# An octonion feed-forward kernel: the second x unit of a group placed ahead of its second down unit

## The chip, the cores and the metric

The kernel runs on one core of one Trainium2 chip. The metric is the device time of one execution in microseconds (us), median of several runs.

## What is computed

The input x is 2048 rows of 1024 numbers. With xn the layer norm of x, the output is x + attention(xn) + ffn(xn).

```python
scale = jnp.mean(jnp.abs(W))
Wq = scale * jnp.clip(jnp.round(W / scale), -1.0, 1.0)    # ternary weights
M = jnp.einsum('jik,jod->koid', S_OCT, Wq)                # octonion product as a matrix
y = jnp.einsum('...id,koid->...ko', xp, M)
...
h = jax.nn.silu(gate) * up                                # two such products of xn
out = oct_ternary_linear(hp, w_down)                      # a third one of h
...
x = x + _L0_attn_ref(xn) + _L0_ffn_ref(xn, w_gate, w_up, w_down)
```

The attention part takes each row's circular autocorrelation, weights its six largest lags by a softmax and adds the shifted rows. The lag 0 term outweighs the others so far that the result is xn itself; the kernel computes a bound that shows it for the given rows (units F) and has a slow branch for rows where it doesn't hold. So what is written is x + xn + ffn(xn).

## The kernel before

Rows are worked in G = 8 groups of 256. The work is a hand-written list of **units** (lines 51 to 68), and every engine walks that list with its own part of each unit. For group g and chunk c of the hidden layer (NC = 3 chunks of up to 114):

- G (g, c, Y) and U (g, c, Y): gate and up products of one half Y of the octonion parts. Below, G2.1 is ("G", g, 2, 1), and so on.
- N (g, t): the down product of the 128 rows t; N0 and N1 below. In group g's stretch the N units of group g - 1 are worked.
- X (g, i): transposes of the normalised x of group g into the operand tile xop; X0 and X1 below. In group g's stretch those of group g + 1 are worked.
- F (g): the matmuls of the bound.

A G, U or N unit is a fast algorithm with two halves on TensorE. At its place n in the list TensorE runs the **first half** (16 matmuls at line 311 for G and U, 96 at line 336 for N); ScalarE **copies** the odd quarters out of PSUM (`pk`, line 568); VectorE does the **first adds** (lines 734 to 738) and the **second adds** (lines 750 to 782), four instructions each; then TensorE runs the **second half** (line 318 or 336), at place n + 2, behind the first half of the unit there. After it: for G, ScalarE's silu (lines 593 to 596); for U, VectorE's **product** h (line 838) at place n + 2; for N, VectorE's **residual** (lines 849, 850), at place n + 2 too, and SP's store of the finished tile.

An X unit is 8 transposes on TensorE (line 378), a copy and a rounding on ScalarE (562, 563; one more at 579), and a block of VectorE instructions at once (817, 727 to 766, with a fold at 748 for X1), then 871.

Behind a product h, ScalarE rounds it to f16 (line 539, place n + 3), POOL forms sums and differences (lines 990 to 996), ScalarE rounds these (line 526, at the place that the table round_at gives), and POOL computes the two remainders (lines 998, 1001). POOL works the U units strictly in order. Between two of them, at U0.0 of groups 1 to 6, it computes the normalisation factors of the next group (rstd, lines 964 to 977). ScalarE needs these to normalise x (line 464), and VectorE takes two dots of the normalised rows (line 693) ahead of N0's first adds.

The PSUM accumulator has four places, taken in turn: the unit at place n needs what the unit at n - 4 left there to be gone (`bank_free`): for G its silu, for U its product, for X line 871, for N its residual, for F its minimum.

The loop that TensorE walks:

```python
for n in range(N + 2):
    ...                     # bank_free(unit n - 4), then the first half of unit n
    if n >= 2:
        u = units[n - 2]    # then the second half of unit n - 2
```

SP's queue stores tile t of a group once its residual is done, and behind N1's store loads the two x tiles of the group three ahead (load_x, line 259), then the tile for the next residual.

Of the kernel before, what the change touches and what calls it, by code (L numbers as in the profile page):

```python
def octonion_ffn_attention_kernel(nc, x, w_gate, w_up, w_down, dft, lag, out):
# [15 lines left out]
    G = ROWS // T  # L17
# [33 lines left out]
    units = [("T", 0, 0), ("S", 0), ("X", 0, 0), ("X", 0, 1), ("T", 1, 0), ("S", 1)]  # L51
# [4 lines left out]
    for g in range(1, G):  # L56
        for c in range(NC):
            units += [("G", g, c, 0)]
            if c == 1 or c == 2 and g < G - 1:
                units += [("N", g - 1, c - 1)]  # L60
            units += [("U", g, c, 0)]
            if c and g < G - 1:
                units += [("X", g + 1, c - 1)]
            units += [("G", g, c, 1), ("U", g, c, 1)]
            if c == 2 and g < G - 1:
                units += [("F", g + 1)]

    units += [("N", G - 2, 1)] + [("-", i) for i in range(4)] + [("N", G - 1, 0), ("N", G - 1, 1), ("-", 4), ("R",)]
    N = len(units)
    place = {u: n for n, u in enumerate(units)}  # L70
# [40 lines left out]
    round_at, z_at = {}, {}  # L111
    for u in u_no:
        _, g, c, Y = u
        late = 6 if g == 0 or c == 2 else 4 if (c, Y, g) == (1, 0, G - 1) else 5
        if (g, c) == (G - 1, NC - 1):
            late = 4 + 3 * (1 - Y)
        round_at[place[u] + late] = u
    for _, g, t in n_no:
        z_at[place["N", g, t] + (t if g == G - 1 else 1 if t == 0 else 2 if g == G - 2 else 3)] = (g, t)
    bound_at = place["N", G - 1, 1]  # L120

    ctx = ExitStack()
    with ctx:
# [68 lines left out]
        def bank_pair(n, rows=P):  # L192
            return acc[0:rows, n % 4, :, :]
# [434 lines left out]
        def _(dve):  # L628
# [59 lines left out]
            def dot(g, t):  # L688
                k = NT * g + t
                dve.wait_ge(norm_done, NT * g + NT)  # L690
                if k:
                    dve.wait_ge(dot_done, k)
                nc.vector.scalar_tensor_tensor(dj[:, :], xr[:, t, 0:D // 2], 1.0, xr[:, t, D // 2:D], ALU.mult, ALU.mult,
                                               accum_out=dots[:, k:k + 1]).then_inc(dot_done, 1)
# [22 lines left out]
            def first_adds(n, u):  # L717

                kind, q = u[0], quad_no[u]
                (p0, p1, p2, _), (o1, o3), (b, d) = quad_parts(n, u)  # L720
                if kind == "X" and u[2] == 1:
                    b, d = d, b
                dve.wait_ge(copied, q + 1)
                if q >= 2:
                    dve.wait_ge(y_done, 4 * q - 4)
                if kind == "X":
                    nc.vector.scalar_tensor_tensor(b, p2, XS, o3, ALU.mult, ALU.add).then_inc(l1_done, 1)
                    dve.wait_ge(xlo_done, x_no[u] + 1)
                    nc.vector.scalar_tensor_tensor(p1, p0, XS, o1, ALU.mult, ALU.subtract).then_inc(l1_done, 1)
                    nc.vector.scalar_tensor_tensor(d, p2, XS, o3, ALU.mult, ALU.subtract).then_inc(l1_done, 1)  # L730
                    dve.wait_ge(l1_done, 4 * q + 2)
                    nc.vector.scalar_tensor_tensor(p0, p0, XS, o1, ALU.mult, ALU.add).then_inc(l1_done, 1)
                else:
                    nc.vector.tensor_tensor(b, p2, o3, ALU.add).then_inc(l1_done, 1)  # L734
                    nc.vector.tensor_tensor(p1, p0, o1, ALU.subtract).then_inc(l1_done, 1)
                    nc.vector.tensor_tensor(d, p2, o3, ALU.subtract).then_inc(l1_done, 1)
                    dve.wait_ge(l1_done, 4 * q + 2)
                    nc.vector.tensor_tensor(p0, p0, o1, ALU.add).then_inc(l1_done, 1)  # L738
# [71 lines left out]
            for n in range(N + 2):  # L810
                u = units[n] if n < N else ("",)
                kind = u[0]
                if kind == "X":
                    four = bank_pair(n).rearrange("p b (i t) -> p (b i) t", t=T)
                    at = 4 * u[2]
                    dve.wait_ge(xhi_done, x_no[u] + 1)
                    nc.vector.scalar_tensor_tensor(xop[:, u[1] % 2, at:at + 4, 1, :], four, XS, xop[:, u[1] % 2, at:at + 4, 0, :], ALU.mult, ALU.subtract).then_inc(xlo_done, 1)  # L817
                if u == ("T", 0, 0):
                    dve.wait_ge(w_in[0], 64)
                    half = NJ * NC * DB // 2  # L820
                    nc.vector.tensor_reduce(asum[0:CH, 0, 0:1], stage[0][0:CH, 0:half], AX.X, ALU.add, apply_absolute_value=True).then_inc(abs_done[0], 1)
                    dve.wait_ge(ln_done, 1)
                    nc.vector.tensor_scalar(xr[:, 1, :], xr[:, 1, :], nm[:, 1:2], rs[:, 1:2], ALU.add, ALU.mult).then_inc(norm_done, 1)
                if n in norm_at and kind == "N":
                    dot(norm_at[n], 0)
                    dot(norm_at[n], 1)
                if kind and kind in "GUNX":
                    first_adds(n, u)
                if kind == "X":
                    second_adds(n, u)  # L830
                if n >= 2:
                    v = units[n - 2]
                    if v[0] == "U":
                        m = u_no[v]
                        dve.wait_ge(term_mm, prod_no[v] + 1)
                        dve.wait_ge(silu_done, m + 1)
                        if m < LAST:
                            nc.vector.scalar_tensor_tensor(hx[0:CH, m % 4, :, :], hx[0:CH, m % 4, :, :], (hsc, nhsc)[v[3]][0:CH, :],  # L838
                                                           bank_pair(n - 2, CH).rearrange("p b (i t) -> p (b i) t", t=T), ALU.mult, ALU.mult).then_inc(h_done, 1)
                        else:  # L840
                            split_last(v)
                    elif v[0] == "N":
                        _, g, t = v
                        pair = bank_pair(n - 2).rearrange("p b e -> p (b e)")
                        res = zx[:, t, :]
                        most = D - DB
                        dve.wait_ge(term_mm, prod_no[v] + 1)
                        dve.wait_ge(z_done, n_no[v] + 1)
                        nc.vector.scalar_tensor_tensor(res[:, 0:most], pair[:, 0:most], osc[:, :], res[:, 0:most], ALU.mult, ALU.add)
                        nc.vector.scalar_tensor_tensor(res[:, most:D], pair[:, most:D], nosc[:, :], res[:, most:D], ALU.mult, ALU.add).then_inc(out_done, 1)  # L850
                    elif v[0] == "F":
                        dve.wait_ge(lag_mm, f_no[v] + 1)
                        nc.vector.tensor_reduce(dmin[:, NT * v[1]:NT * v[1] + NT], acc[:, (n - 2) % 4, 1, :].rearrange("p (t l) -> p t l", t=NT),
                                                AX.X, ALU.min).then_inc(bound_done, 1)
                if kind and kind in "GUN":
                    second_adds(n, u)
                if kind == "S":
                    thresholds(n, u[1])
                    if u[1] == 0:
                        up_scales()  # L860
                    if u[1] == 2:
                        out_scales()
                if kind == "R":
                    dve.wait_ge(flag_mm, 1)
                    nc.vector.tensor_copy(flag[:, :], acc[:, n % 4, 0, 0:1]).then_inc(flag_done, 1)
                if 1 <= n <= N:
                    v = units[n - 1]
                    if v[0] == "X":
                        at = NJ + 4 * v[2]
                        dve.wait_ge(xhs_done, x_no[v] + 1)  # L870
                        nc.vector.tensor_tensor(xop[:, v[1] % 2, at:at + 4, 1, :], bank_pair(n - 1).rearrange("p b (i t) -> p (b i) t", t=T),  # L871
                                                xop[:, v[1] % 2, at:at + 4, 0, :], ALU.subtract).then_inc(x_ready, 1)
                    if v[0] == "T":
                        weight_slots(n - 1, v)
                if n in dot_at:
                    dot(*dot_at[n])
                if n == bound_at:
                    bound()
# [158 lines left out]
```

## Time and profile before

| | |
|---|---|
| median of 3 runs | 638.65 us (638.45 to 638.71) |
| the profiled execution | 638.42 us |
| span of its instructions | 636.6 us |
| mean granted TensorE clock | 0.962 |
| busy: PE, DVE, POOL, ACT | 559.4 (88%), 540.0 (85%), 457.6 (72%), 357.2 (56%) |
| chain that ended last, by engine | POOL 47%, issue 28%, DVE 9%, PE 9%, ACT 4% |

Times in the rows count from the span's start. PE is TensorE, DVE VectorE, ACT ScalarE, POOL GpSimd, SP the queue that issues the DMAs. A timeline row gives start, duration, engine, line, operation and, in brackets, how long the engine was idle before it and whose result ended that. The start of the next instruction on an engine can lie some 0.1 us before the printed end of the one ahead, since they are pipelined. Groups 1 to 6 are steady: the same rows come back 67.33 us later. Group 3's stretch of the list shows all of it: G2.0 starts at 312.02, F at 337.66, and G2.0 of the next group at 379.35.

### The profile page before, as it was taken

Reading aid. Unit: us, or ns where it says so; the run is one execution under the profiler, and the core shown is the slowest. Engines: PE = TensorE matmul, PEld = TensorE weight load, DVE = VectorE, ACT = ScalarE, POOL = GpSimd, SP = SyncE. Lnnn points to the kernel's source line nnn. Section 1 sums busy time; section 2 is a strip of 40 time slices with the busy share of each in tenths; the row PEclk is TensorE's granted clock in tenths of the full one; section 3 lists DMA queues with packets and bytes.
Section 4 is the critical chain, followed back from the end, with each engine's and each line's share of the span. In section 5 each row is a group of like instructions: output and inputs, shape, how many; then the busy total and the mean of one; then the engine's idle time right before and its main releaser. Section 6 shows DMA issues by size and latency. Waiting matters only on the chain.

```text
span 636.6 us, 15791 instructions
## 1 busy us (share of the span) xinstructions
PE 559.4 (88%) x6416; PEld 506.8 (80%) x6416; DVE 540.0 (85%) x1293; ACT 357.2 (56%) x503; POOL 457.6 (72%) x356
## 2 busy tenths in 40 slices
PE   0495846938999999999999999999999999999996
PEld 0374634727998899989998999899989998899896
DVE  1998779898989988998988898989899889976864
ACT  4757364537545764586547665575467545553441
POOL 2004837465967999599977997699779986987930
PEclk9777988969999999999999999999999999999999
DMA  9420002001023001120203010300130011002021
GB/s 234 112 68 0 1 1 67 1 0 68 2 68 132 3 2 68 52 83 3 67 2 133 3 60 8 134 1 22 49 133 1 3 67 43 27 2 67 2 69 67
DMA packets 10233, 30.63 MB, mean 48 GB/s; under 512 B 912, under 2 KB 4016, under 8 KB 10160
## 3 DMA queue, kind: packets, MB, share of 16 engines
q1 hardware_dynamic: 9200, 28.22, 13.5%
q10 hardware_dynamic: 960, 1.40, 0.9%
q8 instruction: 50, 0.82, 0.6%
q14 instruction: 23, 0.19, 0.1%
HBM read 21.23 MB, written 8.39 MB: 47 GB/s over the span
## 4 chain that ended last, share of the span: by engine, by line
POOL 47%; issue 28%; DVE 9%; PE 9%; ACT 4%; DMA 1%; POOLq 0%; SPq 0%; ACTq 0%; DVEq 0%
POOL hop L1001 13%; POOL hs L995 9%; POOL hs L996 8%; POOL hs L991 8%; POOL hs L990 6%; PE acc L336 5%; PE acc L318 2%; PE acc L311 2%; DMA xr<-in_x 1%; DVE zx L671 1%; POOL r L966 1%; DVE wd L685 1%; DVE hx L838 1%; ACT junk L459 1%; DVE xop L817 1%
## 5 line engine op out<-in xcount | busy, mean ns | idle before, releaser
L336 PE MATMUL acc<-wd,hop 114*128 114x128 f16 (+1 forms) x2944 | 169.6, 219 | 0.3 <-DVE acc L756 0.2
L336 PEld LDWEIGHTS acc<-wd,hop 114*128 114x128 f16 (+1 forms) x2944 | 166.6, 98 | 1.4 <-DVE acc L756 0.8
L990 POOL TENSOR_TENSOR hs<-hx 114x512 f32<-114x512 f32 x47 | 60.1, 1279 | 94.7 <-DVE hx L838 93.9
L1001 POOL TENSOR_TENSOR hop<-hs,hop 114x1024 f16<-114x1024 f32 x46 | 98.5, 2141 | 36.6 <-ACT hop L526 36.6
L311 PE MATMUL acc<-xop,wg 128*128 128x256 f16 x768 | 98.1, 285 | 19.5 <-DVE zx L671 10.3
L318 PE MATMUL acc<-xop,wg 128*128 128x256 f16 x768 | 94.9, 278 | 16.7 <-DVE acc L774 11.5
L568 ACT ACTIVATE pk<-acc 114x512 f32<-114x512 f32 (+1 forms) x112 | 65.7, 588 | 68.5 <-PE acc L336 34.9
L311 PEld LDWEIGHTS acc<-xop,wg 128*128 128x128 f16 x768 | 77.0, 102 | 32.7 <-DVE zx L671 10.8
L318 PEld LDWEIGHTS acc<-xop,wg 128*128 128x128 f16 x768 | 75.6, 100 | 29.7 <-DVE acc L774 12.5
L998 POOL TENSOR_TENSOR hop<-hx,hop 114x1024 f16<-114x1024 f32 x46 | 99.1, 2154 | 0.0
L311 PE MATMUL acc<-xop,wu 128*128 128x256 f16 x768 | 93.6, 276 | 3.7 <-DVE xop L871 2.9
L318 PE MATMUL acc<-xop,wu 128*128 128x256 f16 x768 | 91.8, 273 | 3.9 <-DVE acc L774 2.9
L539 ACT ACTIVATE hop<-hx 114x1024 f16<-114x1024 f32 x46 | 48.6, 1056 | 73.9 <-DVE hx L838 73.9
L734 DVE TENSOR_TENSOR bd<-acc,pk 114x256 f32<-114x256 f32 (+1 forms) x112 | 47.0, 420 | 48.1 <-ACT pk L568 48.1
L311 PEld LDWEIGHTS acc<-xop,wu 128*128 128x128 f16 x768 | 75.8, 99 | 14.1 <-DVE xop L871 3.2
L318 PEld LDWEIGHTS acc<-xop,wu 128*128 128x128 f16 x768 | 73.8, 98 | 14.6 <-DVE acc L774 3.6
L526 ACT ACTIVATE hop<-hs 114x1024 f16<-114x1024 f32 x46 | 48.5, 1055 | 46.9 <-POOL hs L996 46.9
L838 DVE SCALAR_TENSOR_TENSOR hx<-hx,few,acc 114x1024 f32<-114x1024 f32 x47 | 59.8, 1272 | 6.4 <-PE acc L318 3.3
L995 POOL TENSOR_TENSOR hs<-hs 114x512 f32<-114x512 f32 x47 | 62.4, 1328 | 3.7
L996 POOL TENSOR_TENSOR hs<-hs 114x512 f32<-114x512 f32 x47 | 62.4, 1328 | 0.0
L991 POOL TENSOR_TENSOR hs<-hx 114x512 f32<-114x512 f32 x47 | 60.0, 1277 | 0.0
L738 DVE TENSOR_TENSOR acc<-acc,pk 114x256 f32<-114x256 f32 (+1 forms) x112 | 47.3, 422 | 0.0
(133 smaller groups left out, 824.3 us busy)
## 6 DMA issues: line engine op xcount, KB each, us to landing
xr<-in_x SPq DMA_DIRECT2D x16, 512.0 KB, 4.8
zx<-in_x SPq DMA_DIRECT2D x16, 512.0 KB, 3.7
out_y<-zx SPq DMA_DIRECT2D x16, 512.0 KB, 2.9
hop<-in_w_down SPq DMA_DIRECT2D x1, 1364.0 KB, 18.1
hop<-in_w_gate ACTq DMA_DIRECT2D x1, 1152.0 KB
hop<-in_w_up SPq DMA_DIRECT2D x1, 1152.0 KB
hop<-in_w_gate ACTq DMA_DIRECT2D x1, 192.0 KB
hop<-in_w_up SPq DMA_DIRECT2D x1, 192.0 KB
```

The lines of the kernel that those rows point to most:

```text
L311: last = nc.tensor.matmul(acc[:, n % 4, s // 2, T * (s % 2):T * (s % 2 + 1)], wm[:, c, slot, :], xop[:, g % 2, form, level, :], start=s // ...
L318: last = nc.tensor.matmul(acc[:, n % 4, s // 2, T * (s % 2):T * (s % 2 + 1)], wm[:, c, slot, :], xop[:, g % 2, form, level, :], start=Fals ...
L336: last = nc.tensor.matmul(acc[:, n % 4, s // 2, at:at + P], operand(g, c, t, form, level), wd[0:WIDE[c], slot, c, :], start=which == 0 and ...
L539: nc.scalar.activation(half_of(g, c, 4 * Y, 0), by_tile(h), ACT.Copy).then_inc(hhi_done, 1)
L568: nc.scalar.activation(pk[0:rows, q % 2, :, :], pair[0:rows, :, T:2 * T], ACT.Copy).then_inc(copied, 1)
L838: nc.vector.scalar_tensor_tensor(hx[0:CH, m % 4, :, :], hx[0:CH, m % 4, :, :], (hsc, nhsc)[v[3]][0:CH, :], bank_pair(n - 2, CH).rearrange( ...
L990: nc.gpsimd.tensor_tensor(hs[:, 4:8:2, :], h[:, 0:4:2, :], h[:, 1:4:2, :], ALU.add)
L991: nc.gpsimd.tensor_tensor(hs[:, 5:8:2, :], h[:, 0:4:2, :], h[:, 1:4:2, :], ALU.subtract).then_inc(hpair_done, 1)
L995: nc.gpsimd.tensor_tensor(hs[:, 0:2, :], hs[:, 4:6, :], hs[:, 6:8, :], ALU.add).then_inc(hs_done, 1)
L996: nc.gpsimd.tensor_tensor(hs[:, 2:4, :], hs[:, 4:6, :], hs[:, 6:8, :], ALU.subtract).then_inc(hs_done, 1)
L998: nc.gpsimd.tensor_tensor(half_of(g, c, 4 * Y, 1), by_tile(h), half_of(g, c, 4 * Y, 0), ALU.subtract).then_inc(h_free, 1)
L1001: nc.gpsimd.tensor_tensor(half_of(g, c, NJ + 4 * Y, 1), by_tile(hs[:, 0:4, :]), half_of(g, c, NJ + 4 * Y, 0), ALU.subtract).then_inc(h_rea ...
```

## The change

In the stretch of groups 1 to 6 the part of the list for chunk 2 was G2.0, N1, U2.0, X1, G2.1, U2.1, F; it becomes G2.0, X1, N1, U2.0, G2.1, U2.1, F. The table round_at puts the rounding of U1.0's sums six places behind its unit instead of five, and that of U2.0's sums five behind instead of six, which is the same place of the list as before, since U2.0 itself moved by one. z_at puts ScalarE's preparation of N1's residual (line 515) one place behind N1 instead of three, one place earlier in the list than before. On VectorE the second adds of a G unit now stand ahead of the residual of an N unit two places back: G2.1 in groups 1 to 6, G1.1 in group 7.

```diff
--- before.py
+++ after.py
@@ -56,11 +56,13 @@
     for g in range(1, G):
         for c in range(NC):
             units += [("G", g, c, 0)]
+            if c == 2 and g < G - 1:
+                units += [("X", g + 1, 1)]
             if c == 1 or c == 2 and g < G - 1:
                 units += [("N", g - 1, c - 1)]
             units += [("U", g, c, 0)]
-            if c and g < G - 1:
-                units += [("X", g + 1, c - 1)]
+            if c == 1 and g < G - 1:
+                units += [("X", g + 1, 0)]
             units += [("G", g, c, 1), ("U", g, c, 1)]
             if c == 2 and g < G - 1:
                 units += [("F", g + 1)]
@@ -112,11 +114,13 @@
     for u in u_no:
         _, g, c, Y = u
         late = 6 if g == 0 or c == 2 else 4 if (c, Y, g) == (1, 0, G - 1) else 5
+        if 0 < g < G - 1 and Y == 0 and c:
+            late = 7 - c
         if (g, c) == (G - 1, NC - 1):
             late = 4 + 3 * (1 - Y)
         round_at[place[u] + late] = u
     for _, g, t in n_no:
-        z_at[place["N", g, t] + (t if g == G - 1 else 1 if t == 0 else 2 if g == G - 2 else 3)] = (g, t)
+        z_at[place["N", g, t] + (t if g == G - 1 else 1 if t == 0 or g < G - 2 else 2)] = (g, t)
     bound_at = place["N", G - 1, 1]
 
     ctx = ExitStack()
@@ -826,7 +830,9 @@
                     dot(norm_at[n], 1)
                 if kind and kind in "GUNX":
                     first_adds(n, u)
-                if kind == "X":
+
+                ahead = kind == "G" and n >= 2 and units[n - 2][0] == "N"
+                if ahead or kind == "X":
                     second_adds(n, u)
                 if n >= 2:
                     v = units[n - 2]
@@ -852,7 +858,7 @@
                         dve.wait_ge(lag_mm, f_no[v] + 1)
                         nc.vector.tensor_reduce(dmin[:, NT * v[1]:NT * v[1] + NT], acc[:, (n - 2) % 4, 1, :].rearrange("p (t l) -> p t l", t=NT),
                                                 AX.X, ALU.min).then_inc(bound_done, 1)
-                if kind and kind in "GUN":
+                if kind and kind in "GUN" and not ahead:
                     second_adds(n, u)
                 if kind == "S":
                     thresholds(n, u[1])
```

TensorE, groups 1 to 6 (here group 1), from G2.0's first half to the first F matmul. In this view 311 and 318 are first and second halves (`wg` a G unit, `wu` a U unit), 336 a half of an N unit, 378 an X unit. Before:

```order
L311 MATMUL acc<-xop,wg 128x256 x16
L318 MATMUL acc<-xop,wg 128x256 x16
L336 MATMUL acc<-wd,hop 128x128 x96
L318 MATMUL acc<-xop,wu 128x256 x16
L311 MATMUL acc<-xop,wu 128x256 x16
L318 MATMUL acc<-xop,wg 128x256 x16
L378 MATMUL acc<-ident,xr 128x128 x8
L336 MATMUL acc<-wd,hop 128x128 x96
L311 MATMUL acc<-xop,wg 128x256 x16
L318 MATMUL acc<-xop,wu 128x256 x16
L311 MATMUL acc<-xop,wu 128x256 x16
L389 MATMUL acc<-xop,dft_sb 128x256
```

With the change (its line numbers are 4 higher):

```order
L315 MATMUL acc<-xop,wg 128x256 x16
L322 MATMUL acc<-xop,wg 128x256 x16
L382 MATMUL acc<-ident,xr 128x128 x8
L322 MATMUL acc<-xop,wu 128x256 x16
L340 MATMUL acc<-wd,hop 128x128 x96
L322 MATMUL acc<-xop,wg 128x256 x16
L315 MATMUL acc<-xop,wu 128x256 x16
L315 MATMUL acc<-xop,wg 128x256 x16
L340 MATMUL acc<-wd,hop 128x128 x96
L315 MATMUL acc<-xop,wu 128x256 x16
L322 MATMUL acc<-xop,wu 128x256 x16
L393 MATMUL acc<-xop,dft_sb 128x256
```

The transposes stand directly behind G1.1's second half, ahead of both halves of N1. G2.1's first half now precedes N1's second half, and U2.0's second half comes behind U2.1's first half instead of behind G2.1's.

ScalarE at the same place, from the silu of G1.1. 526 rounds the sums of a U unit, 539 its product; `pk` copies are 568 (128 rows: N1) and 562 (X1), 563 and 579 round x parts, 593 and 594 are the silu of G2.0, 515 prepares N1's residual. Before:

```order
L596 ACTIVATE hx<-acc,few 114x1024 [waits h_free,term_mm]
L526 ACTIVATE hop<-hs 114x2x4x128 [waits hs_done]
L568 ACTIVATE pk<-acc 128x512 [waits spec_mm,l1_done]
L539 ACTIVATE hop<-hx 114x2x4x128 [waits term_mm,h_done]
L568 ACTIVATE pk<-acc 114x512 [waits spec_mm,l1_done]
L593 ACTIVATE hx<-acc,few 114x768 [waits h_free,term_mm]
L594 ACTIVATE hx<-acc,few 114x256
L562 ACTIVATE pk<-acc 128x512 [waits x_mm,l1_done]
L563 ACTIVATE xop<-acc 128x4x256
L515 ACTIVATE zx<-zx,nmrs,onep 128x1024 [waits zx_in1]
L526 ACTIVATE hop<-hs 114x2x4x128 [waits hs_done]
L568 ACTIVATE pk<-acc 114x512 [waits spec_mm,l1_done]
```

With the change:

```order
L600 ACTIVATE hx<-acc,few 114x1024 [waits h_free,term_mm]
L566 ACTIVATE pk<-acc 128x512 [waits x_mm,l1_done]
L567 ACTIVATE xop<-acc 128x4x256
L530 ACTIVATE hop<-hs 114x2x4x128 [waits hs_done]
L543 ACTIVATE hop<-hx 114x2x4x128 [waits term_mm,h_done]
L572 ACTIVATE pk<-acc 128x512 [waits spec_mm,l1_done]
L583 ACTIVATE xop<-acc 128x4x256 [waits y_done]
L597 ACTIVATE hx<-acc,few 114x768 [waits h_free,term_mm]
L598 ACTIVATE hx<-acc,few 114x256
L519 ACTIVATE zx<-zx,nmrs,onep 128x1024 [waits zx_in1]
L572 ACTIVATE pk<-acc 114x512 [waits spec_mm,l1_done]
L530 ACTIVATE hop<-hs 114x2x4x128 [waits hs_done]
```

X1's two instructions come first; the rounding of U1.1's product now stands ahead of N1's copy, and line 583 (579 before) ahead of the silu of G2.0, which was ahead of X1 before.

POOL's instructions and SP's queue keep their order.

## Rows read from the trace of the kernel before

**Rows 1.** Busy time by stretch: span, busy (x instructions) of PE, PEld, DVE, ACT, POOL, granted clock, DMA, GB/s.
```profile
270.33:337.66 67.33, 66.49 (x793) 61.18 (x793) 60.81 (x149) 40.80 (x56) 58.06 (x44) 1.00 0.14 48
```

**Rows 2.** Timeline of PE, group 3: start, us, line, op, out<-in, xcount [idle before <-releaser].
```profile
312.02 1.92 PE L311 MATMUL acc<-xop,wg 128*128 128x256 f16 x16
...
315.52 5.53 PE L336 MATMUL acc<-wd,hop 114*128 114x128 f16 x96
320.88 1.91 PE L318 MATMUL acc<-xop,wu 128*128 128x256 f16 x16
...
335.86 1.91 PE L311 MATMUL acc<-xop,wu 128*128 128x256 f16 x16
...
338.00 0.27 PE L389 MATMUL acc<-fold,dft_sb 128*128 128x256 f16 x1
339.00 1.92 PE L318 MATMUL acc<-xop,wg 128*128 128x256 f16 x16 [0.73 <-DVE acc L782]
...
342.78 1.92 PE L318 MATMUL acc<-xop,wu 128*128 128x256 f16 x16
...
368.68 5.53 PE L336 MATMUL acc<-wd,hop 114*128 114x128 f16 x96
...
379.35 1.92 PE L311 MATMUL acc<-xop,wg 128*128 128x256 f16 x16
```

**Rows 3.** Timeline of DVE, the same stretch.
```profile
315.66 0.42 DVE L776 TENSOR_TENSOR acc<-acc,bd 114x256 f32<-114x256 f32 x1
...
318.31 0.42 DVE L768 SCALAR_TENSOR_TENSOR acc<-acc,bd 114x256 f32<-114x256 f32 x1
...
329.03 1.23 DVE L817 SCALAR_TENSOR_TENSOR xop<-acc,xop 128x1024 f16<-128x1024 f32 x1 [0.28 <-ACT xop L563]
...
333.15 1.14 DVE L849 SCALAR_TENSOR_TENSOR zx<-acc,few,zx 128x896 f32<-128x896 f32 x1
...
336.34 1.27 DVE L838 SCALAR_TENSOR_TENSOR hx<-hx,few,acc 114x1024 f32<-114x1024 f32 x1
...
362.33 0.69 DVE L693 SCALAR_TENSOR_TENSOR dj<-xr 128x512 f16<-128x512 f32 x1 [1.61 <-ACT xr L464]
...
368.14 0.42 DVE L756 TENSOR_TENSOR acc<-acc,bd 128x256 f32<-128x256 f32 x1
...
378.02 1.27 DVE L838 SCALAR_TENSOR_TENSOR hx<-hx,few,acc 114x1024 f32<-114x1024 f32 x1
```

**Rows 4.** Timeline of POOL, the same stretch.
```profile
337.69 1.27 POOL L990 TENSOR_TENSOR hs<-hx 114x512 f32<-114x512 f32 x1 [3.95 <-DVE hx L838]
...
345.89 2.13 POOL L1001 TENSOR_TENSOR hop<-hs,hop 114x1024 f16<-114x1024 f32 x1 [1.03 <-ACT hop L526]
...
359.67 0.22 POOL L977 TENSOR_SCALAR onep<-rs 128x2 f32<-128x2 f32 x1
```

**Rows 5.** Timeline of ACT, the same stretch.
```profile
324.42 1.06 ACT L539 ACTIVATE hop<-hx 114x1024 f16<-114x1024 f32 x1 [2.67 <-DVE hx L838]
325.38 0.58 ACT L568 ACTIVATE pk<-acc 114x512 f32<-114x512 f32 x1
326.33 0.90 ACT L593 ACTIVATE hx<-acc,few 114x768 f32<-114x768 f32 x1 [0.37 <-PE acc L318]
327.13 0.47 ACT L594 ACTIVATE hx<-acc,few 114x256 f32<-114x256 f32 x1
...
334.87 1.02 ACT L579 ACTIVATE xop<-acc 128x1024 f16<-128x1024 f32 x1
...
341.97 1.05 ACT L448 ACTIVATE junk<-xr 128x1024 f16<-128x1024 f32 x1
...
344.78 1.04 ACT L526 ACTIVATE hop<-hs 114x1024 f16<-114x1024 f32 x1
```

**Rows 6.** Timeline of SP in group 3, and line 259 there: time to landing.
```profile
335.02 1.20 SPq L259 DMA_DIRECT2D xr<-in_x  x2
...
DMA to landing us min/median/max: 4.5/4.9/5.4
```

## Prediction

> **What bounds the kernel now.** I read two views in this order: busy time per stretch, then the timeline of one steady group (group 3) on each engine.
>
> The stretch from one F unit to the next is 67.33 us and repeats five times; TensorE is busy 66.49 us of it at granted clock 1.00, its upper level of 2.4 GHz [rows 1]. That looks like a TensorE bound with a little air. The timeline shows the air: the second half of G2.1 starts at 339.00 though the F matmuls are over 0.11 after 338.00, 0.89 us of waiting for the adds of line 782; then the second half of U2.1 should start at 339.00 + 1.75 + 1.75 = 342.50 and starts at 342.78, 0.28 more [rows 2]. (Two halves of sixteen take 312.02 to 315.52, so 1.75 each; a half of N takes 315.52 to 320.88, 5.36; sums of halves below are PE's own starts.) With 0.06 at F, TensorE has about 1.2 us of removable waits a group.
>
> But one loop through POOL takes just as long, and it is the reason why the period is what it is. Follow it: the product of U2.0 (line 838) starts at 336.34 [rows 3] and POOL starts on it at 337.69 after 3.95 us of idleness. POOL's last instruction for U2.0 (line 1001) waits 1.03 for ScalarE's rounding and starts at 345.89; from there to the normalisation factors at 359.67 no POOL row shows a wait [rows 4]. The dots on VectorE wait 1.61 for the rows that ScalarE normalises with those factors (362.33); behind them VectorE is late until the last second adds of N0 at 368.14 and the product of U1.0 at 378.02 [rows 3]. TensorE starts N0's second half at 368.68, 0.54 after the start of that last add (0.42 of work, 0.06 to pass the semaphore, 0.06 spare), and G2.0 at 379.35, 0.06 after the product's end at 378.02 + 1.27 [rows 2]. G2.0 is where this loop began a group before, at 312.02. So both the TensorE sequence and the POOL loop take 67.33, and a gain needs both to be shorter.
>
> **The change, part by part.** No instruction is added or removed; 8 transposes, two ScalarE roundings, VectorE's X block and N1's block change places. Group 3 stands for all six changed groups (1 to 6), whose trace rows repeat.
>
> (a) X1 ahead of N1 on TensorE. G2.0's first half stays at 312.02, G1.1's second at 313.77, and X1 comes at 315.52, over at 316.39 (8 transposes, 0.87). Next is U1.1's second half. Its second adds start at 315.66 and are ready 1.48 later (start of the fourth, 1.00, plus 0.42 and 0.06): 317.14 [rows 3]. A **new wait of 0.75**; N1's 5.36 covered it before. N1's first half then runs 318.89 to 324.25, G2.0's second to 326.00, U2.0's first to 327.75.
>
> (b) VectorE and ScalarE behind it. VectorE has no pause until the second adds of G2.0 (318.31, four adds, 1.33), then does X1 at once: 319.64. The X block takes 329.03 to 333.15, 4.12, so the product of U1.1 starts at 323.76 [rows 3]. ScalarE's table now puts the rounding of U1.1 before the copy of N1, the X1 sums' rounding and the silu of G2.0. Rounding starts 0.03 after the product's end, 325.06; it takes 0.96 to the next instruction, as 324.42 shows against 325.38; the copy 0.48 and the X rounding 0.92 (their rows print 0.58 and 1.02, of which 0.10 overlaps the next); so silu starts at 327.42 and its second part ends 1.27 later, as 326.33 to 327.60 shows: 328.69 [rows 5]. G2.1's first half needs that bank. TensorE is ready at 327.75 and starts at 328.75: a **new wait of 1.00**. Before, N1's second half lay between.
>
> (c) What the two waits and the order do to U2.0. G2.1 ends its first half at 330.50, N1's second at 335.86, U2.1's first at 337.61. Only now comes U2.0's second half; before, it ran directly behind G2.1's first. From the end of the half that is copied ahead of it (G2.1's, 335.86 - 1.75 = 334.11) to the product of U2.0 at 336.34 it takes 2.23 through copy and adds [rows 2, 3]; so the product starts at 339.84 instead of 336.34, **3.50 later**: 1.75 for U2.1's half, 1.75 for the two waits.
>
> (d) What goes away. G2.1's adds now stand ahead of the residual and have N1's second half and more as cover; 0.89 + 0.28 + 0.06 = 1.23 disappear. At U0.0 of the next group TensorE is 1.75 - 1.23 = 0.52 late.
>
> (e) POOL. It is idle before U2.0, so 3.50 passes through to its line 990. Its line 1001 for U2.0 no longer waits: POOL arrives there at 345.89 - 1.03 + 3.50 = 348.36, and ScalarE's rounding of the sums, at 344.78 now [rows 5], would have to come 2.5 later to hold it; what stands ahead of it comes about 1.6 later (part g). So 3.50 - 1.03 = **2.47 later**, and this goes on undiminished through the factors (359.67), the dots, VectorE's unbroken row of adds and the product of U1.0. TensorE meets it in small pieces (about 0.7 at G0.1's first half, 0.1 at U0.1's, 1.1 at N0's second). I take 2.45 a group.
>
> (f) Where it counts. The factors are made by POOL in the groups after groups 1 to 5: 5 x 2.45 = 12.2. Behind group 6 there is no normalisation; what reaches the end is TensorE's own lateness. It is 1.3 if the pieces at G0.1 and U0.1 (0.7 and 0.1) come on top of 0.52, and 0 if waits that the last group has anyway swallow it; without ScalarE's row sums in that group the two pieces mostly go, so I take 0.5. The last group's G1.1 adds ahead of a residual save nothing: VectorE waits for TensorE there.
>
> (g) Queues. SP sends out N1's tile at the residual's end, then the next two x tiles (335.02, 1.20 for both) [rows 6]. The residual starts at 333.15 now and will start at 336.07 (N1's second half over at 335.86, 0.21 to pass), so the x tiles are issued 2.92 later, at 337.94, and land 4.5 to 5.4 later, at 342.4 to 343.3 [rows 6]. ScalarE sums their rows behind the rounding of U2.0, which starts 1.30 after its product, at 341.14, takes 0.96, and is followed by a squaring of copy size (about 0.5) and a silu (about 1.0): 343.6 instead of 341.97 [rows 5], 1.6 later and just in time. If the tiles are late, up to 1 us a group is added. POOL and PE issue no DMA; the residual's own scaling on ScalarE (z, one place earlier) has its data long before.
>
> **Sum.** The profiled execution took 638.42; 638.42 + 12.2 + 0.5 = 651.1. The median of the runs is 0.23 above it: 651.3.
>
> **Bounds.** From below: if silu of G2.0 did not hold G2.1, TensorE would bring the product of U2.0 only 2.50 later and POOL 1.47: 5 x 1.47 + 0.5, 646.3. From above: x tiles late by 1 us in five groups and 1.3 at the end: 657. VectorE and POOL durations could shift where they overlap (the rows repeat to 0.03 us over the groups), so I don't widen for that.
>
> **Rivals.** (1) TensorE alone sets the pace, and its air is what counts: six times 1.23 is 7.4, giving 631.3. This is **faster**, its place is G2.1 behind F, and it decides if POOL can take the product of U2.0 3.5 us later without passing it on and if silu of G2.0 is in time. For it: TensorE is the busiest engine [rows 1]. Against: G2.0 at 379.35 and N0 at 368.68 stand within 0.06 of VectorE's results [rows 2], and POOL's waits end at 345.89. The Trainium skill (Perfetto Trace Analysis, Optimization Strategy) says to find the gaps on the most-contended engine and make what they wait for start sooner; read that way it speaks for this rival. 6 in 100. (2) POOL's delay is absorbed but TensorE's own 0.52 a group stays: 6 x 0.52 = 3.1, giving 641.8; it needs 2.5 us of slack between 345.89 and 378.02, and the rows show none. 7 in 100. (3) The new order is so close to balance that the waits cancel, within 0.2% (1.3 us, about what a measurement of this kernel tells from no change): 2 in 100. The order of the built program does move as said, so "no change at all" is no rival.
>
> **Chances.** Forecast with its bounds 85 in 100. The range 645.5 to 655.5 reaches from the lower bound to most of the late x tiles. Faster 0.06, within 0.2% 0.02, slower 0.92.
>
> **What would show it.** In the changed profile: 69.8 us from F to F instead of 67.33; no wait at the second half behind F; a wait of 0.75 at U1.1's second half behind the transposes, of 1.0 at G2.1's first half on silu; POOL idle about 6.8 us before U2.0 and not at all at its line 1001; a wait of about 1.1 at N0's second half. Wrong it is if the period is 66.1 (rival 1) or 67.85 (rival 2), or if POOL's factors come less than 2 us later against G2.0 than now.

## The result and the profile after

| | before | after |
|---|---|---|
| median of the runs | 638.68 us (638.45 to 640.20, 4 runs) | 651.73 us (651.16 to 652.97, 4 runs) |
| the profiled execution | 638.42 us | 651.16 us |
| span, mean granted TensorE clock | 636.6 us, 0.962 | 649.3 us, 0.958 |

The ratio is 1.0201, 95% interval 1.0188 to 1.0214: slower by 2.0%, 0.4 us above the forecast 651.3. The two profiled executions are 12.74 us apart.

The page after, busy time by engine and the chain that ended last:

```profile
PE 562.2 (87%) x6416; PEld 505.3 (78%) x6416; DVE 539.4 (83%) x1293; ACT 354.7 (55%) x503; POOL 457.5 (70%) x356
POOL 46%; issue 30%; DVE 11%; PE 8%; ACT 3%; DMA 2%; ACTq 0%; POOLq 0%; DVEq 0%
```

No engine has more work than before: DVE, ACT and POOL are within 2.5 us of their old busy time, and PE runs the same 6416 matmuls (its 2.8 us more are explained below). The busy shares fall and the span grows, so the loss is all waiting. The chain was 47% POOL before and is 46% now.

A stretch of one period after (columns as in [rows 1]; it begins and ends 0.25 ahead of an F):

```profile
274.40:344.13 69.73, 67.16 (x794) 61.03 (x793) 60.70 (x149) 40.41 (x55) 58.04 (x44) 1.00 0.14 47
```

It was 67.33 and is 69.73, still at granted clock 1.00. The 0.67 more that PE shows as busy is no work: the printed end of a row lies some 0.17 behind the place where the next one can start (1.92 against 1.75), and this tail shows as busy wherever the next matmuls come late.

Timeline of PE after, group 3 (its G2.0 starts at 317.06; to compare with [rows 2]):

```profile
317.06 1.92 PE L315 MATMUL acc<-xop,wg 128*128 128x256 f16 x16
...
320.56 1.04 PE L382 MATMUL acc<-ident,xr 128*128 128x128 f32 x8
322.18 1.92 PE L322 MATMUL acc<-xop,wu 128*128 128x256 f16 x16 [0.58 <-DVE acc L786]
...
331.05 1.91 PE L315 MATMUL acc<-xop,wu 128*128 128x256 f16 x16
333.77 1.92 PE L315 MATMUL acc<-xop,wg 128*128 128x256 f16 x16 [0.81 <-ACT hx L598]
...
344.71 0.27 PE L393 MATMUL acc<-fold,dft_sb 128*128 128x256 f16 x1
344.82 1.91 PE L322 MATMUL acc<-xop,wg 128*128 128x256 f16 x16
...
348.31 1.91 PE L322 MATMUL acc<-xop,wu 128*128 128x256 f16 x16
...
352.94 1.92 PE L315 MATMUL acc<-xop,wg 128*128 128x256 f16 x16 [0.53 <-DVE hx L844]
...
372.42 1.91 PE L322 MATMUL acc<-xop,wg 128*128 128x256 f16 x16
374.75 1.09 PE L382 MATMUL acc<-ident,xr 128*128 128x128 f32 x8 [0.42 <-DVE hx L844]
376.08 5.54 PE L340 MATMUL acc<-wd,hop 114*128 114x128 f16 x96 [0.25 <-DVE acc L760]
```

The wait behind F is gone (344.71 to 344.82). In its place stand five: at U1.1's second half, on silu at G2.1's first half, and in pieces printed as 0.25 to 0.53 at G0.1, X0 and N0. By the starts, with the tail of 0.17 counted as waiting, TensorE waits 3.6 us a group instead of 1.2, and the difference is the growth of the period.

DVE and POOL after, the same stretch (line 844 is the product, 996 to 1007 are POOL's part of a U unit, 983 ends the factors):

```profile
344.86 1.27 DVE L844 SCALAR_TENSOR_TENSOR hx<-hx,few,acc 114x1024 f32<-114x1024 f32 x1
```

```profile
337.29 2.13 POOL L1007 TENSOR_TENSOR hop<-hs,hop 114x1024 f16<-114x1024 f32 x1
346.21 1.28 POOL L996 TENSOR_TENSOR hs<-hx 114x512 f32<-114x512 f32 x1 [6.80 <-DVE hx L844]
...
353.35 2.12 POOL L1007 TENSOR_TENSOR hop<-hs,hop 114x1024 f16<-114x1024 f32 x1
...
367.13 0.22 POOL L983 TENSOR_SCALAR onep<-rs 128x2 f32<-128x2 f32 x1
```

POOL stands idle for 6.80 before U2.0 instead of 3.95 [rows 4], no longer waits at its last instruction for that unit, and ends the factors 50.07 behind G2.0's start (367.13 - 317.06), where it was 359.67 - 312.02 = 47.65: 2.42 later. The period grew by 2.40.

### The profile page after: what moved, and what is told of

Same layout as the page of the kernel before. It is cut to its first block, busy times and chain, and to the rows that moved or that the text cites. A ratio compares the mean times of both kernels' runs of the same rounds, so it can differ in the third digit from the quotient of the medians.

```text
span 649.3 us, 15791 instructions
## 1 busy us (share of the span) xinstructions
PE 562.2 (87%) x6416; PEld 505.3 (78%) x6416; DVE 539.4 (83%) x1293; ACT 354.7 (55%) x503; POOL 457.5 (70%) x356
## 4 chain that ended last, share of the span: by engine, by line
POOL 46%; issue 30%; DVE 11%; PE 8%; ACT 3%; DMA 2%; ACTq 0%; POOLq 0%; DVEq 0%
POOL hop L1007 13%; POOL hs L1001 8%; POOL hs L1002 8%; POOL hs L997 8%; POOL hs L996 5%; PE acc L340 5%; PE acc L322 2%; DMA hop<-in_w_gate 2%; DVE zx L675 1%; DVE wd L689 1%; POOL r L972 1%; DVE hx L844 1%; PE acc L315 1%; DVE xop L821 1%; DVE xop L877 1%
```

## The experiments

"Loop" below is the way through POOL that the prediction follows: product of U2.0, POOL, factors, U1.0's product, G2.0, and so to the next U2.0. The edits to the kernel before or after are stated each time; ratios are to the kernel before, which ran beside each (medians 639.1 to 639.8). Since that kernel itself differs by 1.1 us from one set of runs to another, small differences are read from the period in the trace and not from the medians.

**1 and 2. One POOL instruction twice, inside the loop and outside it** (kernel before, nothing moved; the doubled sum goes to the same place). Run 1, where run 2 has (1, 1) for (2, 1):

```
+                if 0 < g < G - 2 and (c, Y) == (2, 1):
+                    nc.gpsimd.tensor_tensor(hs[:, 4:8:2, :], h[:, 0:4:2, :], h[:, 1:4:2, :], ALU.add).then_inc(again, 1)
+                    pool.wait_ge(again, g)
```

> The kernel before, with POOL's first sum of U2.1 computed twice (one more instruction of about 1.3 us) in groups 1 to 5; it stands in the stretch in which POOL never waits before it makes the normalisation factors. Theory (the loop through POOL, the factors and the dots sets the period): every us of it shows, 5 x 1.3 = 6.5, about 645.2. Rival (TensorE's own sequence sets the period before the change): TensorE waits for nothing of it, 638.7.

> The same extra instruction in the same five groups, but in U1.1's block, behind which POOL idles 3.95 us. Loop theory: nothing, 638.7. If what counts is POOL's total work and not its place, it costs the same as the one in U2.1's block, about 645.

Run 1: 645.50, ratio 1.0103 (1.0086 to 1.0120), period 68.67. Run 2: 639.72, ratio 1.0008 (0.9998 to 1.0017), not told apart from before, period 67.34. The same five instructions cost 1.3 us a group, 1.0% in all, in U2.1's block and nothing in U1.1's, where POOL is idle for 3.95 behind them (2.60 in run 2). PE of run 1 shows where the added time reaches TensorE; compare the last two rows of the timeline after:

```profile
410.50 1.92 PE L318 MATMUL acc<-xop,wg 128*128 128x256 f16 x16 [0.73 <-DVE acc L782]
440.13 1.09 PE L378 MATMUL acc<-ident,xr 128*128 128x128 f32 x8 [0.67 <-DVE hx L838]
441.47 5.54 PE L336 MATMUL acc<-wd,hop 114*128 114x128 f16 x96 [0.25 <-DVE acc L756]
```

X0 and N0's second half wait as in the changed kernel, with no unit moved. So a later POOL passes on whole, though POOL is busy only 72% of the span and TensorE 88%. This is what the sum needed.

**3. U2.0's sums rounded one place later** (kernel after):

```
-            late = 7 - c
+            late = 6
```

> The changed kernel, with only ScalarE's rounding of U2.0's sums put one place later (six behind its unit instead of five) in groups 1 to 6. TensorE waits for this rounding nowhere nearby. Loop theory: POOL's last instruction for U2.0 starts about 3.2 us later, and 5 groups make 16: about 667.7. Rival (the change costs what TensorE waits at U1.1 and G2.1, POOL only follows): no change, 651.7.

Measured 672.48, ratio 1.0515 (1.0494 to 1.0536): 20.8 over the kernel after, where 16 was expected. POOL's wait is there:

```profile
439.25 2.13 POOL L1007 TENSOR_TENSOR hop<-hs,hop 114x1024 f16<-114x1024 f32 x1 [3.21 <-ACT hop L530]
```

From one F to the next it takes 72.97 in one group (354.06 to 427.03), 3.24 more than 69.73, as this wait says. In the four others it takes 74.35 to 74.58. Their extra 1.4 to 1.6 stands in N0's second half:

```profile
387.67 1.09 PE L382 MATMUL acc<-ident,xr 128*128 128x128 f32 x8 [2.77 <-DVE hx L844]
389.01 5.54 PE L340 MATMUL acc<-wd,hop 114*128 114x128 f16 x96 [0.25 <-DVE acc L760]
...
460.64 1.15 PE L382 MATMUL acc<-ident,xr 128*128 128x128 f32 x8 [2.77 <-DVE hx L844]
461.98 6.94 PE L340 MATMUL acc<-wd,hop 114*128 114x128 f16 x96 [0.19 <-DVE acc L760]
```

The same 96 matmuls take 6.94 in place of 5.54. The busy time of these two stretches in the same run (seventh number: granted clock):

```profile
389.00:394.37 5.37, 5.36 (x96) 5.36 (x97) 5.14 (x14) 2.75 (x5) 5.29 (x5) 1.00 0.00 0
461.97:468.75 6.78, 6.77 (x96) 6.77 (x97) 6.53 (x17) 3.06 (x6) 6.70 (x6) 0.78 0.01 4
```

In this run TensorE's clock falls behind these waits, in four groups of five. Without that the loop gives 651.7 + 5 x 3.24 = 667.9, where the loop theory said 667.7. The profiled execution adds up: it took 673.30, 22.1 more than that of the kernel after, which is 16.2 for the loop and 1.4 to 1.6 in each of four groups for the clock. In the kernels before and after the clock stays at 1.00 in the steady groups, so this plays no part in the result. It also shows that the move of U2.0's rounding to place 5, a part of the change, is needed.

**4. The dots taken from N0's place to N1's** (kernel after):

```
+        dots_at[place["N", b - 1, 1]] = g
...
-                if n in norm_at and kind == "N":
-                    dot(norm_at[n], 0)
-                    dot(norm_at[n], 1)
+                if n in dots_at:
+                    dot(dots_at[n], 0)
+                    dot(dots_at[n], 1)
```

> The changed kernel, with VectorE's two dots taken from ahead of N0's first adds to ahead of N1's, where VectorE idles about 1.7 us. Loop theory: N0's adds no longer stand behind the factors plus 2.3 us of dots but only behind ScalarE's normalisation, 1.8 us earlier, and VectorE's backlog before U1.1 shrinks: period about 67.9, 642 to 644. Rival (TensorE's own new waits): only U1.1's wait of 0.75 could go, 6 x 0.75 = 4.5, 647.2.

Measured 646.06, ratio 1.0107 (1.0090 to 1.0124): 5.7 less than after, near neither forecast. The period is 68.82, 0.91 shorter, not by the whole 2.3 that the dots take. ScalarE after and then in this run says why:

```profile
367.38 2.38 ACT L468 ACTIVATE xr<-xr,nmrs,rs 128x1024 f32<-128x1024 f32 x2 [1.81 <-POOL onep L983]
...
373.32 1.06 ACT L530 ACTIVATE hop<-hs 114x1024 f16<-114x1024 f32 x1 [1.95 <-POOL hs L1002]
374.72 1.06 ACT L543 ACTIVATE hop<-hx 114x1024 f16<-114x1024 f32 x1 [0.34 <-DVE hx L844]
375.69 0.58 ACT L572 ACTIVATE pk<-acc 114x512 f32<-114x512 f32 x1
```

```profile
365.34 2.37 ACT L469 ACTIVATE xr<-xr,nmrs,rs 128x1024 f32<-128x1024 f32 x2 [1.80 <-POOL onep L984]
...
370.38 1.06 ACT L531 ACTIVATE hop<-hs 114x1024 f16<-114x1024 f32 x1 [1.06 <-POOL hs L1003]
371.35 1.04 ACT L544 ACTIVATE hop<-hx 114x1024 f16<-114x1024 f32 x1
372.29 0.58 ACT L573 ACTIVATE pk<-acc 114x512 f32<-114x512 f32 x1
```

After, the copy of U1.0 (the last row) starts 8.31 behind the normalising, here 6.95. The rounding of line 543 no longer waits for VectorE, but both roundings, and the copy behind them, still stand behind POOL's sums of U0.0. Of the 1.36 only 0.9 arrives at U1.0's product, because a second branch of the loop leads there: from POOL's sums of U0.1 through ScalarE's rounding of them to the copy of G1.1, whose adds stand ahead of that product. This copy and VectorE's first add behind it, after and then in run 4:

```profile
383.52 0.58 ACT L572 ACTIVATE pk<-acc 114x512 f32<-114x512 f32 x1
...
384.13 0.42 DVE L738 TENSOR_TENSOR bd<-acc,pk 114x256 f32<-114x256 f32 x1
```

```profile
380.58 0.58 ACT L573 ACTIVATE pk<-acc 114x512 f32<-114x512 f32 x1
...
381.19 0.42 DVE L739 TENSOR_TENSOR bd<-acc,pk 114x256 f32<-114x256 f32 x1 [0.44 <-ACT pk L573]
```

The copy reaches VectorE 0.61 after its start in both. After, VectorE is done with the work ahead of it at that very moment and shows no wait: the two branches are equally long to a few hundredths. In run 4 the branch that had held the dots is 0.44 early and the one through POOL's sums and ScalarE sets the time. That this one became shorter as well, by 0.89 from the factors to the copy (383.52 - 367.13 against 380.58 - 365.08), is POOL's doing. Its two last sums of U0.0, after and then here:

```profile
369.89 1.72 POOL L1001 TENSOR_TENSOR hs<-hs 114x512 f32<-114x512 f32 x1
371.58 1.71 POOL L1002 TENSOR_TENSOR hs<-hs 114x512 f32<-114x512 f32 x1
```

```profile
367.85 1.27 POOL L1002 TENSOR_TENSOR hs<-hs 114x512 f32<-114x512 f32 x1
369.08 1.27 POOL L1003 TENSOR_TENSOR hs<-hs 114x512 f32<-114x512 f32 x1
```

After, both sums begin while the dots run on VectorE (369.79 to 372.17), and take 1.72 instead of 1.27. In run 4 the dots run from 327.95, and there it is two sums of U1.1 that take 1.65 and 1.72, ahead of POOL's idle time. So the 0.9 a group is what the dots cost POOL, not what they cost VectorE. Why the two engines slow each other is not shown here. The prediction named only the branch through the dots.

**5. Silu of G2.0 ahead of the X1 rounding on ScalarE** (kernel after; the four lines of the rounding put behind the silu block):

```
-                if 1 <= n <= N and units[n - 1][0] == "X":
...
+                if 1 <= n <= N and units[n - 1][0] == "X":
...
```

> The changed kernel, with ScalarE's silu of G2.0 ahead of the rounding of the X1 sums (0.92 us). Loop theory: G2.1's wait on that silu shrinks from 1.0 to about 0.1, the product of U2.0 comes 0.9 earlier and with it POOL, 5 groups and the last one: 5 x 0.92 + 0.5, about 646.5. Rival (POOL's lateness of 2.45 is there whatever TensorE does at G2.1, since POOL idles anyway): 651.7.

Measured 646.03, ratio 1.0102 (1.0082 to 1.0121), as forecast. The period is 68.82, the wait of 0.81 on line 598 is gone, and no other wait takes its place.

**6. The adds of G2.1 and G1.1 behind the residual again** (kernel after, `ahead = False`):

> The changed kernel, with the second adds of a G unit behind the residual again, as the kernel before has them. VectorE comes about 0.3 later to U2.1's first adds and so to the product of U2.0. Loop theory: 5 x 0.33, about 653.4. Rival (this swap is what costs): clearly faster than 651.7.

Measured 653.27, ratio 1.0216 (1.0198 to 1.0234); 653.4 was forecast. The two intervals overlap, and the periods say how much this part of the change saves: 69.94 against 69.74 (F to F), 0.20 a group and 1.0 us in five, less than the 0.33 forecast. That the time still fits the forecast is partly luck: in the profiled execution a lower clock in group 1 (last section) adds another 1.1 us (75.87 from its factors to the next, where the kernel after takes 74.58).

**7. Three edits together**: 4 and 5, and the first row sum moved from F's place to G0.0's, beside the second.

> The changed kernel, with the dots ahead of N1's adds, the silu of G2.0 ahead of the X1 rounding, and ScalarE's first row sum behind the copy of G0.0 instead of ahead of it. Loop theory: the loop through POOL, the normalisation and N0's copy is still there and only 0.92 a group shorter than with the dots moved alone (646.06): about 641.5. Rival (TensorE's waits one by one are what costs): its waits left are 0.75, 0.1 and 0.1 a group, under the 1.23 of the kernel before, so about 636.

Measured 646.44, ratio 1.0115 (1.0098 to 1.0133), where 641.5 was expected: a miss, no better than run 4 alone. The period is 68.39; run 9 takes the miss apart.

**8. Run 7, with the normalising behind N0's copy, the scaling of the residual and the rounding of U0.0's sums one place later.**

> As the one with dots, silu and row sum moved, and besides ScalarE normalises behind N0's copy instead of ahead of it, prepares N0's residual one place later and rounds the sums of U0.0 one place later. Loop theory: POOL's factors then reach TensorE only through the X0 transposes, which have microseconds to spare, so the loop is cut and TensorE's own waits are left: period 66.3 to 67.1, 634 to 638, under the kernel before. Rival (VectorE or ScalarE is simply full): no better than the three moves without this, about 641.

Measured 665.51, ratio 1.0417 (1.0398 to 1.0436): far off. POOL shows the reason:

```profile
314.28 2.13 POOL L1009 TENSOR_TENSOR hop<-hs,hop 114x1024 f16<-114x1024 f32 x1 [2.90 <-ACT hop L530]
...
334.29 2.14 POOL L1009 TENSOR_TENSOR hop<-hs,hop 114x1024 f16<-114x1024 f32 x1 [1.37 <-ACT hop L530]
```

POOL's in-order block of a unit waits at its last instruction for ScalarE's rounding, and what was taken out of ScalarE's queue came back as two waits of POOL. The period is 71.3 to 71.6. TensorE's clock falls here too, to a mean of 0.66 to 0.84 in stretches of 5 us in four of the five groups, but the fifth, at 1.00 throughout, takes 71.33 as well, so the clock is not what costs.

**9. Runs 4 and 5 together, without the row sum.**

> The changed kernel with the dots ahead of N1's adds and silu ahead of the X rounding, row sums left where they are. The run with both and the row sums together took 646.44 with a steady period of 68.40 against 68.82 for the dots alone, but its group 1 made its factors 1.8 us late behind the two sums. If that is the whole of the miss, this kernel keeps the 68.40 and loses the 1.8: 646.1 - 5 x 0.42 = 644.0 (between 643.3 and 644.6). A wait of about 0.3 at N1's second half then stands where the 0.8 on silu stood, since the dots now hold N1's adds. Rival A: silu's whole 0.8 a group counts, 641.5. Rival B: silu gives nothing once the dots are moved, 646.

Measured 645.51 (643.61 to 645.53), ratio 1.0086 (1.0068 to 1.0105), above the 643.3 to 644.6 expected. The steady period is 68.41, 0.41 less than in run 4, and the wait on silu has become the smaller one that was expected:

```profile
402.31 5.54 PE L341 MATMUL acc<-wd,hop 114*128 114x128 f16 x96 [0.31 <-DVE acc L761]
```

But the sum over the whole run is only 0.85 below run 4 (profiled executions 645.49 and 646.34), where 0.41 a group would give over 2. The reason that I had expected, row sums in group 1, is not it, since this kernel has them in their old place. Busy time by stretch at the start of group 1, first in run 4, then in this run (columns as before):

```profile
150.00:155.00 5.00, 4.99 (x46) 4.49 (x47) 5.00 (x13) 1.55 (x3) 2.05 (x8) 1.00 0.02 5
```

```profile
150.00:155.00 5.00, 4.99 (x31) 3.86 (x32) 5.00 (x13) 1.55 (x3) 2.06 (x8) 0.66 0.02 5
```

In both, TensorE is busy for the whole stretch and starts it at the same time, but it starts 46 matmuls in the one and 31 in the other. N0's first half starts at 155.26 in run 4 and at 156.93 in this one: 1.67 lost once, to the clock. Taken off, run 9's profiled execution would be at 643.8, and 646.34 - 643.8 = 2.5 is six times 0.41. One run of the four, at 643.61, lies there; its mean granted clock was 0.967, that of the three others 0.954 to 0.959. That the difference lies in group 1 is likely, but only one execution of a kernel has a trace. Run 7's trace has the same 0.66 there; its row sums cost a further 0.8 (span 644.5 against 643.7). So the miss of run 7 has three parts: the dots, which now stand ahead of N1's adds, leave 0.31 of the 0.81 a group in place; the clock; and the row sums.

**10 to 12. Is there something for the kernel before?** Run 10 takes the dots out of its loop as in run 4. Run 11 puts G2.1's second adds ahead of U2.0's product on VectorE, so that TensorE need not wait behind F. Run 12 does both.

```
+                ahead = kind == "G" and 0 < u[1] < G - 1 and u[2:] == (2, 1)
-                if kind == "X":
+                if ahead or kind == "X":
                     second_adds(n, u)
...
-                if kind and kind in "GUN":
+                if kind and kind in "GUN" and not ahead:
                     second_adds(n, u)
```

> The kernel before with only the dots moved behind, ahead of N1's adds. Theory of two bounds: in the kernel before TensorE's own order (66.49 busy plus about 0.8 of waiting for G2.1's second adds behind F) already fills the period, so a shorter POOL loop gives no more than the 0.06 spare at G2.0: 638.4, no difference that can be measured. Rival: the POOL loop alone sets the period before, then it gains what it gained in the changed kernel, 0.9 a group: 634.

> The kernel before with G2.1's second adds ahead of U2.0's product on VectorE in groups 1 to 6, nothing moved on TensorE. TensorE's waits behind F (0.89 and 0.28) go; POOL gets U2.0's product 1.33 later, of which its wait of 1.03 at the rounding takes 1.0. Theory of two bounds: the loop is 0.3 longer, 5 x 0.3 = 1.5: 640.2 (639 to 641). Rival, TensorE alone sets the pace: 6 x 1.17 less, 631.7.

> Both edits: the dots taken out of the POOL loop (0.9 a group shorter, as measured on the changed kernel) and G2.1's second adds ahead of U2.0's product (0.3 longer there, TensorE's waits behind F gone). Theory of two bounds: both bounds fall, the loop to 67.33 - 0.9 + 0.3 = 66.7 and TensorE below it, 5 x 0.6 less: 635.7 (634.5 to 637), faster than either kernel, though each edit alone brings nothing. Rival: the dots hold N1's second half as in the changed kernel (0.3 a group), 637.2.

Run 10: 639.73, ratio 1.0000 (0.9988 to 1.0011), as forecast. The period is 67.33 as before, and POOL now has air at U1.0, where before it had none (its sums beside the dots' old place take 1.27 again, not 1.72):

```profile
379.03 1.27 POOL L991 TENSOR_TENSOR hs<-hx 114x512 f32<-114x512 f32 x1 [1.02 <-DVE hx L839]
```

So with the loop made a microsecond shorter the kernel gains nothing, and with the loop 1.3 longer (run 1) it loses 1.3 a group: the kernel before stands on both bounds at once, as the prediction said.

Run 11: 642.85, ratio 1.0055 (1.0042 to 1.0068); 640.2 was expected. Run 12: 643.45, ratio 1.0059 (1.0046 to 1.0073); 635.7 was expected. Both have a period of 67.90, and PE of run 11 shows one cause for both:

```profile
408.44 0.28 PE L389 MATMUL acc<-xop,dft_sb 128*128 128x256 f16 x1 [1.22 <-DVE hx L839]
...
412.80 1.92 PE L318 MATMUL acc<-xop,wu 128*128 128x256 f16 x16 [0.26 <-DVE acc L782]
```

F is four places behind U2.0 and takes its place in PSUM, which the product has to empty first. The adds that went ahead of the product hold it up by 1.33, and TensorE now waits 1.22 ahead of F where it waited 0.73 behind it (both as printed). Moving the dots cannot help there, so run 12 is no faster than run 11. I had looked for the product's readers on POOL and had not asked who takes its bank. No version tried beats the kernel before.

## Why the prediction was right

Point by point, against the timelines above:

- **(a)** U1.1's second half starts 0.75 after the transposes are over (322.18 - 320.56 - 0.87); 0.75 was forecast.
- **(b)** G2.1's first half starts 0.97 after TensorE was ready (333.77 - 331.05 - 1.75); 1.00 was forecast. Run 5 takes this wait alone away and gets 5.7 us back.
- **(c)** U2.0's product starts 27.80 behind G2.0 (344.86 - 317.06), before 24.32: 3.48 later, forecast 3.50.
- **(d)** U2.1's second half, at 348.31, is 31.25 behind G2.0, before 342.78 - 312.02 = 30.76: TensorE is 0.49 late, forecast 0.52. It is N1's second half, now ahead of this one, that covers G2.1's adds; their place on VectorE has no part in it, since run 6, with the adds behind the residual, has the same 31.25 (350.06 - 318.81).
- **(e)** POOL idle 6.80, forecast 6.8; factors 2.42 later, forecast 2.47. The pieces on TensorE: G0.1 0.70 by the starts (forecast 0.7), X0 and N0's second half together 1.04 by their starts (0.58 and 0.46), forecast 1.1 at N0 alone. The place was slightly off: the transposes of X0 wait too, since they take the bank that the product of line 844 empties.
- **(f)** The row at the end of the factors comes 0.23 later than before in group 1 (153.06 against 152.83) and 12.25 later in group 6 (506.60 against 494.35): 12.02 in five groups, forecast 12.2. Behind it 0.51 is added up to the last matmul (642.47 against 629.71), forecast 0.5; that this fits so closely is luck, since the prediction took it from between 0 and 1.3.
- **(g)** The x tiles were not late: their row sum starts 31.54 behind G2.0 (348.60), forecast 31.58, with no wait ahead of it.

Rival 1, TensorE alone sets the pace, falls twice: by the result, and by run 1, in which TensorE's order is untouched. The rule that the Trainium skill gives (Perfetto Trace Analysis, Optimization Strategy), to close the gaps of the most-contended engine, was followed at the gap behind F by this change and by run 11. Both closed it (0.73 as printed, 0.89 by the starts), and both kernels became slower, by 13.0 and 3.4 us in the medians. The trace does not bear it out where a loop through a less busy engine takes as long. Rival 2, that POOL's delay is absorbed, falls by run 1 and by the factor rows.

What the prediction had incomplete is the way behind the factors. It named the dots, "VectorE's unbroken row of adds" and the product of U1.0. The row is not unbroken: behind N0's adds VectorE waits 0.27 in the kernel before and 0.28 after for ScalarE's copy of U1.0. And a second branch, through POOL's sums of U0.1 and ScalarE's queue, is just as long (run 4). It did not matter for this change, which delays both alike, but it made the forecast of run 4 too good.

## What to carry to other kernels

Before a gap on the busiest engine is closed by a move, follow the results that come later through the other engines until they return to it: if that loop has the same period, its delay counts whole and the gap was worth nothing. A cheap test is to double one small instruction of the suspected loop and, for comparison, one elsewhere on the same engine. When instructions change places, ask for each result that becomes later both who reads it and who waits for the memory that it frees, and compare the durations of what now runs beside them on another engine.

## What was not expected of the hardware

Waits have a second price through TensorE's clock. In run 3, N0's first half waits 0.73 for an operand from POOL and X0 waits 2.77 some 10 us later. In the group at 461.97 the granted clock of the half that follows is 0.78, a mean between the levels of 1.2 and 2.4 GHz, which costs 1.40; one group with the same waits kept 1.00. In group 1 of run 9, behind a stretch in which TensorE waited 7.4 and 3.4 us, the clock is 0.66 for 5 us and costs 1.67, where run 4, which waited 8.2 and 3.0, has 1.00. The waits that bring it down and those that don't are close together here, and no run tells them apart. The traces of runs 5 to 8 show 0.66 at the same place, those of the kernels before and after do not. So a profiled execution can differ from another by this step of 1 to 2 us alone, and differences of that size are better read from the steady groups.
